# Queries as three 16-bit parts, and VectorE instructions over two steps, in the fused attention stage of a graph kernel

## The reference

```
h = relu(layernorm(x));  Q, K, V = h @ Wq, h @ Wk, h @ Wv        # 8 heads of 32
score = einsum('ehd,ehd->eh', Q[dst], K[src]) / sqrt(32)
score = score + relu(efeat @ W1 + b1) @ W2 + b2                   # from 64 edge features
m = segment_max(score, dst);  ex = exp(score - m[dst])
alpha = ex / segment_sum(ex, dst)[dst]
out = segment_sum(alpha[:, :, None] * V[src], dst) @ Wo + bo
```

## Time and profile before

| | |
|---|---|
| median of 3 runs | 5708.9 us |
| profiled execution | 5703.44 us, of which span 5701.6 us |
| PE busy | 4929.3 us (86%) |
| DVE busy | 3404.5 us (60%) |
| ACT busy | 3304.3 us (58%) |
| POOL busy | 3201.2 us (56%) |
| fused stage | about 300 to 2880 us of the span |

### The profile page before, as it was taken

The page is one execution under the profiler, slowest core; times in us unless marked ns, Lnnn a source line. Parts: engine busy times, 40 slices in busy tenths (PEclk is TensorE's granted clock), DMA queues, the critical chain, the costliest instruction groups (busy, mean ns, idle before and its releaser), DMA issues. The chain is left out here.

```text
span 5701.6 us, 116421 instructions
## 1 busy us (share of the span) xinstructions
PE 4929.3 (86%) x22946; PEld 3002.5 (53%) x22947; DVE 3404.5 (60%) x7904; ACT 3304.3 (58%) x8030; POOL 3201.2 (56%) x3311
## 2 busy tenths in 40 slices
PE   4899999999999999999879999967777677667665
PEld 3566666666666666666534444444444444444443
DVE  3289999999999999999943333333333333333333
ACT  1488888888888888888634444333333333333332
POOL 1156666666666666666700000077777777777775
PEclk8999999999999999999989999966666766776776
DMA  2477777777777777777734444433333333333334
GB/s 84 146 209 221 222 222 223 221 224 221 221 224 221 222 222 223 219 223 222 215 117 141 141 141 141 142 105 105 105 105 105 105 105 105 105 105 105 105 105 126
DMA packets 627599, 929.53 MB, mean 163 GB/s; under 512 B 161869, under 2 KB 464079, under 8 KB 627536
## 3 DMA queue, kind: packets, MB, share of 16 engines
q0 software_dynamic: 208384, 648.75, 39.2%
q1 hardware_dynamic: 419152, 280.06, 16.8%
HBM read 795.60 MB, written 132.88 MB: 163 GB/s over the span
## 5 line engine op out<-in xcount | busy, mean ns | idle before, releaser
L919 POOL DMA_INDIRECT kv_rows<-kv_d,idx x1664 | 1663.9, 1000 | 935.8 <-PE sums L1096 462.3
L1651 PE MATMUL m_sums<-m_rows,m_oh 128*128 x3328 | 1393.1, 567 | 584.8 <-ACT m_rows L1633 510.0
L1594 POOL DMA_INDIRECT m_rows<-msg_d,m_idx x1568 | 1485.7, 947 | 507.5 <-issue 434.7
L1633 ACT ACTIVATE m_rows<-m_rows,m_norm 128x256 f32<-128x256 f32 x1568 | 710.8, 500 | 1265.6 <-DMA m_rows<-msg_d,m_idx 1265.6
L1651 PEld LDWEIGHTS m_sums<-m_rows,m_oh 128*128 128x128 f32 x3328 | 839.9, 276 | 1138.1 <-issue 1015.0
L1674 DVE TENSOR_TENSOR agg<-agg,m_sums 128x256 f32 x832 | 350.6, 421 | 1315.6 <-PE m_sums L1651 1312.0
L1096 PE MATMUL sums<-kv_rows,onehot 128*128 128x264 f32 x3328 | 934.0, 404 | 10.2 <-DVE kv_rows L1221 3.5
L1057 PE MATMUL p_q<-q,pickT 128*128 x3328 | 869.4, 384 | 13.3 <-ACT pickT L962 9.4
L1096 PEld LDWEIGHTS sums<-kv_rows,onehot 128*128 128x128 f32 x3328 | 574.6, 190 | 384.9 <-issue 313.6
L939 ACT ACTIVATE hid<-p_hid,b1s 128x512 f32<-128x512 f32 x784 | 495.7, 683 | 373.4 <-PE p_hid L1035 373.4
L1529 PE MATMUL p_m<-wr,h1T 128*128 128x512 f32 x1568 | 710.7, 597 | 0.0
(11 more groups left out here) (181 smaller groups left out, 4451.0 us busy)
## 6 DMA issues: line engine op xcount, KB each, us to landing
msg_d<-msg SPq DMA_DIRECT2D x196, 512.0 KB
dsts<-dstrow_d SPq DMA_DIRECT2D x416, 128.0 KB
ef_raw<-in_edge_attr_dram SPq DMA_DIRECT2D x195, 256.0 KB
kv_rows<-kv_d,idx POOLq DMA_INDIRECT x1664
m_rows<-msg_d,m_idx POOLq DMA_INDIRECT x1568
kv_d<-kvo SPq DMA_DIRECT2D x49, 260.0 KB
pens<-pens_d SPq DMA_DIRECT2D x104, 96.2 KB
emlp<-mlp_d SPq DMA_DIRECT2D x104, 64.0 KB
```

The lines of the kernel that those rows point to most:

```text
L919: pool.indirect_dma_start(rows[:, u, k, :], None, kv_d[:, :], bass.IndirectOffsetOnAxis(idx[:, half, c:c + 1], 0)).then_inc(gathered[u], 16)
L1594: pool.indirect_dma_start(rows[:, u, k, :], None, msg_d[:, :], bass.IndirectOffsetOnAxis(idx[:, u // 2, c:c + 1], 0)).then_inc(gathered[u] ...
L1633: last = nc.scalar.activation(rows[:, u, k, :], rows[:, u, k, :], ACT.Copy, scale=norm[:, bass.ds(2 * g + k, 1)])
L1651: last = nc.tensor.matmul(sums[u % BANKS][:, 0:D], onehot[:, u % HOTS, k, :], rows[:, bass.ds((groups + RING - 1) & (RING - 1), 1), k, :]. ...
```

## The change

The queries are kept as three bf16 numbers a value (a bf16 value, the bf16 of what is left, the bf16 of what is then left), side by side in one tensor `shelf` of 50 x 768 bf16 numbers a partition. Block n's queries stand in row n+1, its running sums in row n of the same tensor, read as f32; so a block's sums stand where the queries of the block before it stood. `pickT` becomes bf16. `select` issues six bf16 matmuls in place of two f32 ones. The sums of a block aren't cleared beforehand: the first `add` of a block multiplies the old content by zero, with a number read from a new table `keep`.

DVE's product of queries and keys is written over the keys in `kv_rows`; the head sums and the weighing are one instruction for two steps. ACT takes over `first_node`, with two instructions a chunk. In the projections DVE makes the second and third part of the queries, with three instructions a block, and PE waits for the first of them before it reuses a PSUM slot.

```diff
@@ node_projections, DVE
+            def split(i, j):
+                n = B * i + j
+                dve.wait_ge(q0_ready, n + 1)
+                nc.vector.scalar_tensor_tensor(out=qr[:, j, :], in0=qq[SLOT[j]][:, 0:D], scalar=HD ** -0.5, in1=q_part(0, n),
+                                               op0=ALU.mult, op1=ALU.subtract).then_inc(qr_ready, 1)
+                if not (first and j < 1):
+                    second(n - 1, (j - 1) % B)
+                if not (first and j < 2):
+                    third(n - 2, (j - 2) % B)
+            def second(n, j):
+                dve.wait_ge(qr_ready, n + 1)
+                nc.vector.tensor_copy(q_part(1, n), qr[:, j, :]).then_inc(q1_ready, 1)
+            def third(n, j):
+                dve.wait_ge(q1_ready, n + 1)
+                nc.vector.tensor_tensor(q_part(2, n), qr[:, j, :], q_part(1, n), ALU.subtract)
             def iteration(i, more):
                 for j in range(B):
+                    split(i, j)
                     if more:
...
@@ attend, PE, select
-                    last = nc.tensor.matmul(p_q[u % 2][:, k * D:(k + 1) * D], pickT[:, u % PICKS, k * P:(k + 1) * P],
-                                            q[:, bass.ds(b, 1), :], start=True, stop=True)
+                    for part in range(3):
+                        last = nc.tensor.matmul(p_q[u % 2][:, k * D:(k + 1) * D], pickT[:, u % PICKS, k * P:(k + 1) * P],
+                                                q[:, bass.ds(b, 1), part * D:(part + 1) * D].rearrange("p b d -> p (b d)"),
+                                                start=(part == 0), stop=(part == 2))
...
@@ attend, DVE, dot
-                nc.vector.tensor_tensor(prod[:, :, :], p_q[u % 2][:, :].rearrange("p (k d) -> p k d", k=2), rows[:, u, :, 0:D],
+                nc.vector.tensor_tensor(keys, p_q[u % 2][:, :].rearrange("p (k d) -> p k d", k=2), keys,
                                         ALU.mult).then_inc(prod_done, 1)
+                if (u + 1) % DOTS == 0:
+                    nc.vector.tensor_reduce(dots[:, x, :, r:r + DOTS, :].rearrange("p k r h -> p r k h"),
+                                            rows[:, a:u + 1, :, 0:D].rearrange("p s k (h c) -> p s k h c", h=H),
+                                            AX.X, ALU.add).then_inc(dots_done, 1)
...
@@ attend, DVE, weigh and add
-                v = rows[:, u, :, D:KV].rearrange("p k (h c) -> p k h c", h=H)
+                v = rows[:, u:u + WEIGHS, :, D:KV].rearrange("p s k (h c) -> p (s k) h c", h=H)
...
-                nc.vector.tensor_tensor(to, to, sums[u % 2][:, 0:KV - D].unsqueeze(1), ALU.add).then_inc(added, 1)
+                nc.vector.scalar_tensor_tensor(out=to, in0=to, scalar=t["keep"][:, bass.ds(s, 1)], in1=sums[u % 2][:, 0:KV - D],
+                                               op0=ALU.mult, op1=ALU.add).then_inc(added, 1)
...
@@ attend, DVE, body
-                    if is_step(s - LATE):
+                    if is_step(s - LATE) and (u - LATE) % WEIGHS == 0:
                         v = u - LATE
                         weigh(s - LATE, v % SLOTS, 2 * i + v // R, (v // R) % 2)
```

More of the change, by code:

```diff
@@ L94, in build @@
         t["ident"] = sb("t_ident", [P, P])
+        t["keep"] = sb("t_keep", [P, TSTEPS])
         t["eps"] = sb("t_eps", [P, 1])
@@ L408, in _ @@
             nc.vector.tensor_copy(t["block"], blkf[:, :])
+            nc.vector.memset(t["keep"][:, 0:1], 0.0)
+            nc.vector.tensor_tensor(t["keep"][:, 1:TSTEPS], nbase[:, 1:TSTEPS], nbase[:, 0:TSTEPS - 1], ALU.is_equal)
             done(nc.vector.memset(moved[:, 0:1], 0.0))
@@ L483, in node_projections @@
         hT = sb("hT", [P, 3, 2, P])
+        qr = sb("qr", [P, B, D])
         kvo = sb("kvo", [P, B, KV])
@@ L577, in loaded, with q_part @@
                     hold(dve, x_in, 16 * X_LOADS * (i + 1), dve_go)
+            def q_part(part, n):
+                return q[:, bass.ds(n, 1), part * D:(part + 1) * D].rearrange("p a d -> p (a d)")
+            def split(i, j):
+                n = B * i + j
+                first = isinstance(i, int) and i == 0
+                dve.wait_ge(q0_ready, n + 1)
[11 more added lines that the diff above has]
+                nc.vector.tensor_tensor(q_part(2, n), qr[:, j, :], q_part(1, n), ALU.subtract)
             def iteration(i, more):
                 for j in range(B):
+                    split(i, j)
                     if more:
@@ L611, in _ @@
             iteration(BATCHES - 2, True)
+            iteration(BATCHES - 1, False)
+            second(BLOCKS - 1, B - 1)
+            third(BLOCKS - 2, B - 2)
+            third(BLOCKS - 1, B - 1)
         @block.scalar
@@ L633, in iteration @@
                     act.wait_ge(proj_ready, n + 1)
-                    nc.scalar.activation(q[:, bass.ds(n, 1), :].rearrange("p a d -> p (a d)"), qq[s][:, 0:D], ACT.Copy,
-                                         scale=HD ** -0.5)
+                    nc.scalar.activation(q[:, bass.ds(n, 1), 0:D].rearrange("p a d -> p (a d)"), qq[s][:, 0:D], ACT.Copy,
+                                         scale=HD ** -0.5).then_inc(q0_ready, 1)
                     if not (isinstance(i, int) and i == 0):
@@ L663, in iteration @@
                     pe.wait_ge(hT_ready, n + 1)
+                    wait(pe, qr_ready, n + 1 - BACK[j])
                     wait(pe, kv_ready, n + 1 - BACK[j])
@@ L699 @@
 PICKS = 4
+DOTS = 2
+WEIGHS = 2
 HOTS2 = 2
@@ L984, in weights, with first_of @@
                 if not (isinstance(c, int) and c < 2):
-                    act.wait_ge(weighed, R * (c - 1))
-                nc.scalar.activation(wgt[:, x, :, :, :].rearrange("p k r h -> p k (r h)"),
-                                     p_back.rearrange("p (k e) -> p k e", k=2), ACT.Exp).then_inc(wgt_ready, 1)
+                    act.wait_ge(weighed, R // WEIGHS * (c - 1))
+                nc.scalar.activation(wgt[:, x, :, :, :].rearrange("p r k h -> p k r h"),
+                                     p_back.rearrange("p (k r h) -> p k r h", k=2, h=H), ACT.Exp).then_inc(wgt_ready, 1)
+            def first_of(c):
+                if not first(c):
+                    act.wait_ge(first_ready, c)
+                nc.scalar.activation(far_first[:, :], t["iota"][0:1, :], ACT.Abs, scale=-1.0,
+                                     bias=t["dst"][0:1, bass.ds(2 * R * c, 1)]).then_inc(far1_ready, 1)
+                act.wait_ge(far1_ready, c + 1)
+                if not first(c):
+                    act.wait_ge(line_down, c)
+                nc.scalar.activation(first_node[:, :], far_first[:, :], ACT.Relu, scale=-1.0,
+                                     bias=t["one"][0:1, 0:1]).then_inc(first_ready, 1)
             def body(i):
@@ L1008, in body @@
                         hot(s - LATE, (u - LATE) % HOTS2)
+                    if u % R == 0 and is_chunk(c):
+                        first_of(c)
                     if u % R == 3 and is_chunk(c):
@@ L1088, in turn_drop, with add_up @@
                 last.then_inc(drop_turned, 1)
-            def add_up(s, u):
+            def add_up(s, u, batch):
                 pe.wait_ge(hot_ready, s + 1)
-                pe.wait_ge(weighed, s + 1)
+                pe.wait_ge(weighed, batch + 1)
                 if not (isinstance(s, int) and s < 2):
@@ L1143, in dot @@
                 dve.wait_ge(gathered[u], 32 * (n + 1))
[L1144 to L1146 removed]
+                keys = rows[:, u, :, 0:D]
+                nc.vector.tensor_tensor(keys, p_q[u % 2][:, :].rearrange("p (k d) -> p k d", k=2), keys,
                                         ALU.mult).then_inc(prod_done, 1)
[L1148 to L1152 removed]
+                if (u + 1) % DOTS == 0:
+                    a, r = u + 1 - DOTS, (u + 1 - DOTS) % R
+                    dve.wait_ge(prod_done, s + 1)
+                    if r == 0 and not (isinstance(s, int) and s < 2 * R):
+                        dve.wait_ge(score_done, n * 2 + u // R - 1)
+                    nc.vector.tensor_reduce(dots[:, x, :, r:r + DOTS, :].rearrange("p k r h -> p r k h"),
+                                            rows[:, a:u + 1, :, 0:D].rearrange("p s k (h c) -> p s k h c", h=H),
+                                            AX.X, ALU.add).then_inc(dots_done, 1)
             def scans(c):
@@ L1161, in scans, with chain @@
                 nc.vector.tensor_tensor_scan(top[:, ::-1], pens[:, 1:GE + 1][:, ::-1], fwd[:, ::-1], -BIG, ALU.add, ALU.max).then_inc(top_done, 1)
-            LINKS = 9
-            def chain(c, s0):
+            LINKS = 8
+            def chain(c):
                 def linked(n, scan=False):
@@ L1252, in body @@
                         elif u % R == 1:
-                            chain(c, R * c)
+                            chain(c)
                         else:
                             drop(c)
-                    if is_step(s - LATE):
+                    if is_step(s - LATE) and (u - LATE) % WEIGHS == 0:
                         v = u - LATE
```

59 lines of the change are left out of this document (29 added, 30 removed).

## The result

The kernel after took 5789.44 us (median of 4 runs, 5786.8 to 5795.61), the kernel before 5707.03 us beside it: a ratio of 1.0146, with a 95% interval of 1.0131 to 1.0161. Slower by 82 us, where I had forecast 46 us faster. The profiled execution has a span of 5786.8 us, 85.2 more than before.

A forecast was written before the change was run, and what follows sets the result against it. PE bounds the fused stage, with DVE close behind. Fused stage -63, projections +16 and the table keep +1 sum to -46 us: 5657 from the profiled 5703.4, 5663 as a median; range 5590 to 5725.

The forecast's parts named there:

- So a chunk is DVE's 22.7 plus 1.7: 24.4 us: Fused stage: a chunk takes DVE's own floor plus its wait in step 6, 24.4 us against 25.0 before.
- The 1.7: Step 6 of a chunk: DVE's add waits 1.7 us for PE's sums.
- The 22.7: DVE's floor for a chunk after the change: 23.4 - 1.0 - 0.2 + 0.5 = 22.7 us.
- The walk: Fused stage: PE and DVE ties followed from step 3's product; DVE waits in step 6, and is late in other steps.
- the 1.0 for the pairs: DVE in the fused stage: two-step head sums and weighings save 0.25 us a pair, 1.0 a chunk; bounds 0 and 1.4.
- The 0.5 that I added for the adds: DVE's adds: a scalar from memory costs 0.06 us each, 0.06 x 8 = 0.5 a chunk (0 to 1.0).
- p_q 0.74: PE in the fused stage: the group of six bf16 matmuls takes 0.74 us where p_q took 0.95.
- short matmuls cost more: Rival on PE's p_q group: at 1.1 us a group, a chunk is 26.2 us and the kernel 5840; chance 0.16.
- loads stand between them: Rival on PE's p_q group: weight loads stand between the matmuls; no size in the text; chance 0.03.
- +16 forecast: Projections: the turn comes 2.7 us late at six batch ends, +16 us; least 10, most 36.
- ACT absorbs its two instructions: ACT in step 0: about 0.7 us a chunk of new work is absorbed; without cover up to 0.7 a chunk.
- PE alone bounds: Rival, fused stage: no DVE wait in step 6, chunk 23.3 us, kernel 5555; chance 0.14 including times between it and the forecast.

The follow-up runs named there:

- two_parts2: Kernel after with p_q made from two of the three bf16 query parts, four matmuls a step instead of six; 5744.73 us, chunk 25.13 us.
- hoist_register2: Kernel after with DVE's block register read once a step right behind the product, not in rescale and add; 5745.64 us, chunk 25.21 us.
- first_node_back: Kernel after with the first_node comparison back on DVE and ACT's two instructions gone; 5792.29 us, chunk 25.65 us.
- w1_single_weigh: Kernel after with the weighing one instruction a step again, head sums still paired; 5720.9 us, ratio to before 1.0032.
- both1_single: Kernel after with both head sums and weighing one instruction a step again; 5682.37 us, ratio to before 0.9963.
- imm_add2: Against the kernel with both pairs undone: DVE's add takes constant 0 instead of the keep value, leaving out earlier steps' sums; 5648.7 us.
- proj_order: Kernel after with the next batch's reciprocal and normalising ahead of the split of blocks 5 and 6 in the projections; 5766.48 us, ratio 1.0106.
- d1_single_headsum: Kernel after with the head sums one instruction a step again, weighing still paired; 5735.79 us, ratio to before 1.0056.

## Why the prediction was wrong

- **"So a chunk is DVE's 22.7 plus 1.7: 24.4 us"** is the step that failed; it measured 25.61. The 1.7 was right (1.62, at 10.80 behind the product of step 3 where I had 10.69), and two_parts2 shows the tie. The 22.7 was wrong, and with it "in the other steps I followed the same ties and found DVE late rather than PE". The walk left 9.7 us for steps 0 to 2: 24.4 less 14.7 for steps 3 to 7 (the add at 10.69, 0.4 to the product of step 7, 3.6 for that step), which measured 14.83 and so were right. Steps 0 to 2 took 10.78.
- Of these 1.1 us, 0.40 is the bare register load in step 2 (hoist_register2), and 0.16 is `first_node`, priced at 0.20 and worth 0.04 (first_node_back). I put the remaining half down to the start of the scores behind the paired head sums. That the scores come 0.55 us later is shown, and so is the scan's wait of 0.63 in w1_single_weigh, which single head sums take away; its share in the kernel after is only read from rows (0.20 at the scan, 0.27 at the add behind it), not measured apart.
- The term of the floor that failed is the 1.0 for the pairs. The late chunks, without the hidden layer on PE, are the ones that gave me the floor of 23.4. There the kernel after takes 23.79 us on the mean (six from 2796.65 to 2939.39, 23.5 to 24.4 each) and not 22.7, and both1_single, with no pairs, 23.83 (2693.02 to 2835.99). Of the 1.0 us that the pairs were to take off the floor next to nothing arrived (0.04), though DVE's busy time there is 0.6 a chunk less (22.43 and 23.06). The granted clock was 0.92 and 0.98 in these two stretches, so the comparison is good to some tenths only; the shortest of the six chunks still took 23.53. With the register load moved (hoist_register2) it is 23.32, so about half of the saving was lost to that load. The 0.5 that I added for the adds was right (imm_add2). I took off every saved microsecond of busy time from a floor that consists of dependences too.
- **Prices.** p_q 0.74: measured 0.75 to 0.79 in front of another shape, and 0.67 where the sums follow (1012.23 to 1012.90). Head sums 1.12: 1.13 to 1.14. Weighing 1.15: 1.17 (recorded for 1.25, which is the 0.08 that the walk added). Add +0.06: 0.06. These were right. The two rivals on p_q (short matmuls cost more, loads stand between them) are out: six matmuls of 256 columns with six loads of 98 ns each went in 0.75 us. In the group at 1009.52 the matmuls start every 0.109 us, and the record of the next load starts 2 ns after the matmul it runs beside (1009.526 and 1009.524); if the six loads, 0.59 in sum, stood between the matmuls, 0.16 of the 0.75 would be left for all six of these. The register instructions were right too: where PE is behind, as at 1009.52, the starts are 0.109 apart in spite of them, and where it had caught up, as at 1002.69, the first three distances are 0.125, 0.124 and 0.116, which is 0.04 more. What I had no row for is the matmul time in the 0.74, and so in the 0.21 and the 1.7 a chunk taken from it: the earlier trace rows, the only bf16 matmuls of before, give 0.213 for 256 columns, and the windows view has a granted clock of 1.00 for them (24.88 to 29.77), as in the fused stage. What the runs showed in its place is 0.109 a matmul, 0.65 for six, and 0.10 on top in front of another shape (0.14 with the 0.04). Before, the four f32 records of p_q start 0.216 apart, 0.86 for four, and 0.09 stands on top in the group's 0.95.
- **The projections.** +16 forecast, +25.9 measured. The turn came 2.42 us late (at 159.53, where 2.80 behind the turn at 154.31 would be 157.11) and not 2.7: the three instructions took 0.87 from start to start (157.96 to 158.83), not 1.15; the reciprocal took 0.23, and the turn came 0.47 behind the first xn (159.06). But the lower clock, which I had put at the range's end ("most 36", with 7 us of it; a stretch of before, 32.46 to 39.29, has 0.50 for 6.8 us), came behind each hole of this profile, for 3.4 us: 1.7 us more for one block, six times 4.2 in all. With fewer such stretches the term is smaller: both1_single has four, and 21.4 instead of 25.9. proj_order shows that the late xn made all but 1.4 of it.
- **ACT absorbs its two instructions** (385 and 401 ns): held; DVE waited 2.5 us for ACT's weights in the whole execution, and taking the two instructions away again (first_node_back) gained nothing. **The messages as before**: held (792.15 and 792.20).
- **"PE alone bounds"** is out: a chunk would have come down to 23.3, and in two_parts2 1.8 us less of PE's work a chunk gave 0.48.
- In the sum: the fused stage -63 forecast and +59 measured. 98 chunks by 1.21 (25.61 less 24.4) are 119, and six late ones by 1.1 (23.8 less 22.7) are 6: 125, against a difference of 122. The rest of the miss is the projections' 10.

That the last phase is 4.1 us longer and the first 4.1 shorter is not explained here; the first phase varied by 9 us between kernels that are alike in it (113.41 and 122.88 to the first turn).

## What to carry to other kernels

Two engines that are tied in each step, as here, need not gain from fewer, longer instructions by what these save, and can lose: the partner gets its data later, so before pairing, follow each reader of the pair's result (here the sums, and the scores too) to the instruction that waits for it, in every step of the loop and not only in the one that looks worst. A busy time saved counts only if the instruction did not stand in a gap that stays, and an instruction taken away can lay bare what it hid, here a register load. And a hole in front of a matmul is priced with and without a stretch at half clock behind it (0.50 for 3.4 us), since both came here.

## What the runs showed of the hardware that I had not expected

- Behind a hole of 2.0 to 2.3 us in PE's work the granted clock often went to 0.50 for 3.4 us (160.26 to 163.67 in the kernel after), but not always: six times out of six in the kernel after and in w1_single_weigh, five in two_parts2, four in both1_single, d1_single_headsum, hoist_register2, first_node_back and imm_add2.
- Six matmuls of 256 columns, each with its own weight load over all 128 rows, started every 0.109 us where PE was behind; the records of the loads (98 ns) lie beside those of the matmuls. The f32 records of the same width, two for each matmul, started every 0.216 us with loads of 190 ns.
- An instruction with a scalar from memory took 482 to 484 ns, the same one with a constant 422.
- A register load in DVE's stream showed no price behind a weighing (in both1_single the add starts 0.60 to 0.67 behind it in most steps, and the weighing alone wants 0.61), and cost 0.3 to 0.4 us a chunk in step 2 of the kernel after, where only short dependent instructions stand before it.
- The kernel before took 5704 us on one chip and 6499 on another. Why is open.
